# An adaptive conv + FFN kernel: the first loads in another order (x chunk 0, bias, x chunks 1 to 3, weights)

## What is computed

```python
# x: (128, 32, 512)   cond: (128, 128)   bias: (32,)
y   = conv1d(x, weight, kernel 9, padding 4, groups 4)      # 32 channels, 8 per group
y   = y + einsum('nd,od->no', cond, c_weight)[:, :, None] + bias[None, :, None]
up   = y @ W_up.T                                           # y as (4096, 512), F = 1376
gate = silu(y @ W_gate.T)
out  = x + (gate * up) @ W_down.T
```

## Time and profile before

| | us |
|---|---|
| median of 3 runs (lowest and highest) | 831.0 (830.52 to 832.48) |
| span of the profiled execution | 829.1 |
| TensorE busy in it | 813.3 (98%) |
| DVE, ACT, POOL busy | 294.0, 183.8, 45.1 |
| HBM read, written | 25.32 MB, 8.39 MB |

### The profile page before, as it was taken

One profiled execution on the slowest core, in us unless ns is written; L12 is line 12 of the kernel. 1 busy time (PEld: TensorE's weight loads), 2 busy tenths in 40 slices (PEclk: granted clock), 3 DMA queues, 4 the chain that ended last, 5 costly groups with the idle time before them and its releaser, 6 DMA issues.

```text
span 829.1 us, 9744 instructions
## 1 busy us (share of the span) xinstructions
PE 813.3 (98%) x3715; PEld 660.8 (80%) x3715; DVE 294.0 (35%) x466; ACT 183.8 (22%) x314; POOL 45.1 (5%) x68
## 2 busy tenths in 40 slices
PE   5989999999999999999999999999999999999998
PEld 4778887888878888788887888788887888878886
DVE  3733444433333222533334222343333322242223
ACT  4821433111121111311112111211112111121111
POOL 2200110101000000011100000010100000000000
PEclk9999999999999999999999999999999999999999
DMA  7252220311113000121112200031111200011001
GB/s 228 72 154 86 78 54 26 126 51 52 26 25 127 1 1 0 53 77 51 51 26 75 78 0 1 1 128 51 51 26 26 101 1 1 0 58 45 1 0 51
DMA packets 54059, 42.75 MB, mean 52 GB/s; under 512 B 5024, under 2 KB 43072, under 8 KB 54016
## 3 DMA queue, kind: packets, MB, share of 16 engines
q1 hardware_dynamic: 54016, 42.12, 17.0%
HBM read 25.32 MB, written 8.39 MB: 41 GB/s over the span
## 4 chain that ended last, share of the span: by engine, by line
PE 95%; DVE 1%; DMA 1%; SPq 1%; ACT 1%; issue 0%; ACTq 0%; DVEq 0%
PE up_ps L552 29%; PE acc L568 29%; PE gate_ps L552 29%; PE conv_ps L516 2%; PE conv_ps L509 2%; PE xt_ps L485 2%; DMA bias_col<-in_fside_S 1%; ACT perm_early L638 1%; SPq L313 0%; DMA down_nat<-in_L_ffn_W_down 0%; DVE xt_lo L755 0%; PE xt_ps L535 0%; DVE res L867 0%; PE conv_ps L535 0%; SPq L350 0%
## 5 line engine op out<-in xcount | busy, mean ns | idle before, releaser
L847 DVE TENSOR_TENSOR act_f<-gate_ps,act_f 128x512 f32<-128x512 f32 (+1 forms) x88 | 60.8, 691 | 339.5 <-ACT act_f L680 339.5
L552 PE MATMUL up_ps<-h_hi,wgu_hi 128*128 128x512 f32 (+1 forms) x352 | 141.9, 403 | 0.0
L552 PE MATMUL up_ps<-h_hi,wgu_lo 128*128 128x512 f32 (+1 forms) x352 | 139.2, 395 | 0.0
L552 PE MATMUL up_ps<-h_lo,wgu_hi 128*128 128x512 f32 (+1 forms) x352 | 139.0, 395 | 0.0
L568 PE MATMUL acc<-wd_hi,g_hi 128*128 128x512 f32 (+1 forms) x352 | 138.8, 394 | 0.0
L552 PE MATMUL gate_ps<-h_lo,wgu_hi 128*128 128x512 f32 (+1 forms) x352 | 137.8, 392 | 0.0
L552 PE MATMUL gate_ps<-h_hi,wgu_hi 128*128 128x512 f32 (+1 forms) x352 | 137.8, 391 | 0.0
L568 PE MATMUL acc<-wd_hi,g_lo 128*128 128x512 f32 (+1 forms) x352 | 137.6, 391 | 0.0
L552 PE MATMUL gate_ps<-h_hi,wgu_lo 128*128 128x512 f32 (+1 forms) x352 | 137.4, 390 | 0.0
L568 PE MATMUL acc<-wd_lo,g_hi 128*128 128x512 f32 (+1 forms) x352 | 137.1, 389 | 0.0
L680 ACT ACTIVATE act_f<-gate_ps 128x512 f32<-128x512 f32 (+1 forms) x88 | 52.6, 598 | 377.7 <-PE gate_ps L552 376.9
(11 more groups left out here) (116 smaller groups left out, 520.0 us busy)
## 6 DMA issues: line engine op xcount, KB each, us to landing
res<-in_x SPq DMA_DIRECT2D x32, 256.0 KB, 3.4
out_y<-res SPq DMA_DIRECT2D x32, 256.0 KB, 2.2
x_in<-in_x SPq DMA_DIRECT2D x13, 512.0 KB, 3.8
stage<-win SPq DMA_DIRECT2D x104, 64.0 KB, 2.0
down_nat<-in_L_ffn_W_down SPq DMA_DIRECT2D x10, 256.0 KB, 3.2
w_early<-in_L_ffn_W_gate SPq DMA_DIRECT2D x6, 256.0 KB, 7.1
w_early<-in_L_ffn_W_up SPq DMA_DIRECT2D x6, 256.0 KB, 7.0
x_first<-in_x SPq DMA_DIRECT2D x3, 512.0 KB, 8.2
```

The costliest lines, as they stand in the source:

```text
L552: mm = pe.matmul(bank[0:w, :], wt[:, i, which, f * P:f * P + w], hv[:, i, :], start=i == 0 and n == 0, stop=i == KC - 1 and n == 2)
L847: dve.tensor_tensor(act_f[0:w, :], gate_ps[0:w, :], act_f[0:w, :], ALU.mult).then_inc(silu_done, 1)
```

## The change

The four bias loads follow x chunk 0 at once, x chunks 1 to 3 come next, and the weight chunks 0 to 11 come after them in their old order. All other engines' programs stay as they are.

```diff
--- before.py
+++ after.py
@@ -341,14 +341,13 @@
             sp.dma_start(cond_nat, cond).then_inc(small_in, LD)
 
             load_x(sp, 0, 0)
+            for g in range(G):
+                sp.dma_start(bias_col[:, g, :], bias[g * CG:(g + 1) * CG].rearrange("(a o b) -> a o b", a=1, b=1)
+                             .broadcast_to([R, CG, 1])).then_inc(bias_loaded, LD)
             for i in range(1, KC):
-                load_w(sp, 2 * i - 2)
-                load_w(sp, 2 * i - 1)
                 load_x(sp, 0, i)
-                if i == 1:
-                    for g in range(G):
-                        sp.dma_start(bias_col[:, g, :], bias[g * CG:(g + 1) * CG].rearrange("(a o b) -> a o b", a=1, b=1)
-                                     .broadcast_to([R, CG, 1])).then_inc(bias_loaded, LD)
+            for v in range(2 * KC - 2):
+                load_w(sp, v)
             for v in range(2 * KC - 2, E):
                 load_w(sp, v)
```

## The result

The changed kernel took 835.5 us in the median of 4 runs (834.7 to 836.2), the kernel before, run beside it, 830.8 (828.8 to 832.5). The medians differ by 4.7 us; the ratio is **1.0063, 95% interval 1.0048 to 1.0079**, some 5.2 us. The prediction was 833.9, with a range of 831.6 to 836.2: the direction and the mechanism hold, the size (2.9 us) was a good deal too small.

A forecast was written before the change was run, and what follows sets the result against it. TensorE's long row of matmuls was taken as the bound, so loads move only its start or clock. A start 2.9 us later, other terms at zero, added to the 831.0 median gave 833.9 us, range 831.6 to 836.2.

The forecast's parts named there:

- ACT has slack: ACT's permutations and Toeplitz splits before the second x block: done at 18.3, TensorE's turned block at 18.9, 0.6 us of slack.
- the bias's gain is covered: DVE's context add, freed 3.5 us earlier, is done near 12.2, before weight chunk 0 lands, so nothing is gained.
- (a): Bias loads right behind x chunk 0: the last lands at 9.9 instead of 13.4, freeing DVE 3.5 us earlier.
- (b): Weight chunks 0 and 1 behind all x chunks: chunk 1 lands at 16.5, TensorE's second x block turn 2.9 us later.
- Rival A: TensorE's clock drop near 48 us missing from most later executions: +1.2 us, 832.2; chance 0.16.
- B: More loss than forecast, by a second clock drop, later speed-up or later weight landings: about +1.7, 835.6; chance 0.13.
- C: Bias loads cheap in their new place, weight chunk 1 lands at 12.3: -1.3 us, 829.7; chance 0.08.
- D: The bias was and stays the bound, nothing else moves: gains 3.5 us, 827.5; chance 0.03.
- (c): Weight chunks 2 to 5 and x chunks 1 to 3 land before they are wanted: cost zero, cover 4.2 us.
- (d): x chunks 2 and 3 block SyncE's queue until near 18, before its staging at 25.0: cost zero.

The follow-up runs named there:

- w01_after_bias: Changed kernel with weight chunks 0 and 1 back ahead of x chunk 1, and 2 to 5 in their old places; ratio to the kernel before 1.0002.
- the last pair: Kernel before without its four bias loads, bias spread by one small matmul, with loads in the old order (0.9939) and in the change's order (0.9998).
- bias_before_x1: Kernel before with only the bias loads moved, ahead of x chunk 1 and behind weight chunks 0 and 1; ratio 0.9984.
- weights_last_only: Changed kernel with the bias loads back behind x chunk 1, all weight chunks still last; ratio to the kernel before 1.0044.
- before_again: The kernel before, unchanged, run once more for a second profile; span 828.1 us.
- bias_small_matmul_old: Kernel before without its four bias loads, old load order; bias loaded as 4 rows of 8 numbers and spread by one 4-column matmul; ratio 0.9939.
- bias_matmul_old_order: Kernel before without its four bias loads, old load order; one row of 32 numbers, added to the context product by single-row matmuls; ratio 0.9978.

## Why the prediction came out as it did

- **The mechanism was right.** POOL's wraps hold the second x block back until weight chunk 1 lands, ACT has slack, the bias's gain is covered: shown by the brackets of the changed kernel's rows, by w01_after_bias, which takes those two chunks back (and four later ones) and lands on 1.0002, and by the last pair, where the order alone costs 4.9 us.
- **The bias's landing (a) was mis-sized.** The step took the 3.8 us between x chunk 1 and the last bias as what the loads cost wherever they stand. Directly behind x chunk 0 it was 6.1 and 5.1 us in the two profiles. x chunk 0 landed 0.4 us earlier than before, so the last bias came at 11.9 and not at 9.9: **2.0 us** of the miss. Over the profiles the last bias came 5.1 to 6.3 us behind the chunk ahead of it with 0.5 MB of chunks in front (four profiles), 4.7 and 5.6 with 1 MB (bias_before_x1, weights_last_only), and 3.8 and 3.7 only with the 1.5 MB of the kernel before. That a longer queue in front hides part of the cost fits this row of numbers; no run shows how.
- **What the 3.8 us are was misread**, without harm to the sum. The prediction calls them an empty queue, but its own trace has 5 GB/s or less only from 9.0 to 11.5 us; from 12.0 on the rate is 287 GB/s and more, while the last bias still has over 1 us to go.
- **The 2 MB behind it (b) were mis-sized.** 6.6 us were forecast up to weight chunk 1 and 8.1 measured, **1.5 us** of the miss. An x chunk took 1.7 to 1.9 us, where two weight chunks of the same bytes, 0.7 us apart, take 1.4, and three x chunks stand here where two did: 0.3 us and more. The rest is the pause of 1.4 us, ahead of weight chunk 1 in one profile and of chunk 0 in the other. The prediction saw such a gap once in two places (1.6 us), gave it half weight, 0.4 us, and laid it to SyncE's issue being held. This reason fails: in weights_last_only SyncE was held 5.89 us at weight chunk 0, which still landed 0.6 us behind x chunk 3 (start, us, the DMA issued):

```profile
7.40 5.89 SPq L290 DMA_DIRECT2D w_early<-in_L_ffn_W_gate  x1
```

  What did run ahead of the gap, in the kernel before too (18.4 to 19.6, the late landing at 21.1), is the 16 KB packet told of above. Its part in it stays open.
- **Together**: weight chunk 1 at 20.0 for 16.5, TensorE's turn at 21.23 for 17.8, 6.3 us later than before and not 2.9. The price of 1.3 us from that landing to the turn was right (19.97 to 21.23). That the time still fell within the range is in part luck: in the second set of runs the medians lie 6.0 us apart (835.5 and 829.6), and 831.0 + 6.0 would be above it.
- **A part of the shift was hidden by chance in the first pair of profiles**: the fall of the clock near 48 us, which the kernel before had in its first profile and the changed one had not. Rival A happened there, but it belongs to the execution, not to the change, as before_again shows. Costing it at nothing was right.
- **The rivals.** B's total (835.6) is nearest to the measured 835.5, and one of its three causes, weight chunks that land later still, is the one that acted, though not because SyncE's queue was held. C and D fell: the bias loads were dearer in their new place, not cheaper.
- **The later weight chunks (c) and SyncE (d)** cost nothing that shows: the shift is 5.7 us at the third x block and no longer grows.

## What to carry to other kernels

Order the first loads by the programs of the engines that use them: a load that is put off also puts off everything that stands behind its first user in that engine's program, here an x block whose data had been there for 14 us. Price a transfer on a shared queue by what stands behind it; a load of single numbers can empty the queue for microseconds, and the cure here was to load a few contiguous rows and spread them on chip. And do not carry a gap from one place of a trace to another as if it were a price: the same four loads cost 1.3 to 2.3 us more directly behind the first chunk than behind the second x chunk, and a pause of 1.4 us went with a packet of another queue.

## What was not expected of the hardware

- Four loads of 128 single numbers (2 KB in all) landed 3.7 to 6.3 us behind the chunk ahead of them, a quarter of the numbers about 1 us behind it, and twice as many came 4.5 us later still. For 2.5 us (kernel before, 9.0 to 11.5) and 3.5 us (changed, 5.5 to 9.0) of this the rate was 5 GB/s or less with 1 MB or more issued behind them.
- In each of the 14 profiles one 16 KB packet of the queue called instruction ran for 1.1 to 1.2 us between 14 and 25 us, and a chunk that landed 1.0 to 1.6 us behind its end was 0.6 to 1.6 us late. That one makes the other is not shown.
- A matmul with one row of contraction takes TensorE as long as one with 128: a pair of 128 columns took 0.72 us for either. Sixteen such instructions with changing sources took from 5.18 to 10.97 us, eight without the change 2.08.
- TensorE turned the second x block at full speed in one kernel alone, bias_small_matmul_old, at 10.53 (0.64 us for four transposes). In the kernels in which it idled before, at 11.9 to 21.2, it took 1.08 to 1.12 us. So it did in bias_matmul_old_order at 13.85 (1.09 us), though TensorE had not been idle there since 5.2, but busy, half of the time up to 10.97 with products of a single row; whether these are the reason no run shows. The granted clock of these slices reads 1.00 in several of the profiles; the duration is what tells.
